# Routed attention: half of each head's weights turned by transfers, values one step later, the low halves of the rest on VectorE

## What is computed

```
ss = sigmoid(x @ Ws); sd = sigmoid(x @ Wd)            # two sets of gates, (b, t, H, E)
ms = _topk_mask(ss, 3); md = _topk_mask(sd, 3)        # three of five experts are kept
q = einsum('bthed,bthe->bhtd', q5, sd * md)           # q5 = x @ Wq, per head and expert
k = einsum('bthed,bthe->bhtd', k5, ss * ms)
v = einsum('bthed,bthe->bhtd', v5, ss * ms)
attn = softmax(einsum('bhid,bhjd->bhij', q * scale, k))
out = einsum('bhij,bhjd->bihd', attn, v)              # then spread over the experts by md and projected by Wo
```

## Time and profile before

| | |
|---|---|
| runs | 2855.82, 2860.48, 2865.31 us |
| profiled execution | 2857.4 us, span 2855.6 us |
| busy over the span | TensorE 88%, its weight load 59%, VectorE 72%, ScalarE 51%, GpSimd 65% |
| mean granted clock of TensorE | 0.951 |
| first scores of stage g0, of stage g1 | 1429.95 us, 2226.42 us after the start |
| step starts (scores of the next step) in g1 | 2249.90 (step 0) to 2821.48 (step 62) |

### The profile page before, as it was taken

The page is one execution under the profiler, slowest core; times in us unless marked ns, Lnnn a source line. Parts: engine busy times, 40 slices in busy tenths (PEclk is TensorE's granted clock), DMA queues, the critical chain, the costliest instruction groups (busy, mean ns, idle before and its releaser), DMA issues. The chain is left out here.

```text
span 2855.6 us, 59345 instructions
## 1 busy us (share of the span) xinstructions
PE 2525.9 (88%) x22659; PEld 1696.9 (59%) x22718; DVE 2049.0 (72%) x3682; ACT 1453.3 (51%) x2071; POOL 1853.3 (65%) x1754
## 2 busy tenths in 40 slices
PE   6787696795999999999689999999797899999997
PEld 3555444553666666666456666666534566666666
DVE  7998446446677677676688888887485888888874
ACT  4222122334888888888334455445362245544554
POOL 1887100003999999999357888887501577888885
PEclk9998798897999999999899999999898999999999
DMA  1000000003998998899300000000101000000000
GB/s 42 1 1 0 22 1 13 22 1 87 155 157 148 150 156 150 149 157 142 87 1 1 2 1 2 2 1 2 30 1 59 1 1 1 2 1 2 2 1 16
DMA packets 362421, 126.25 MB, mean 44 GB/s; under 512 B 344584, under 2 KB 353288, under 8 KB 362144
## 3 DMA queue, kind: packets, MB, share of 16 engines
q1 hardware_dynamic: 362144, 122.46, 23.3%
HBM read 20.70 MB, written 1.05 MB: 8 GB/s over the span
## 5 line engine op out<-in xcount | busy, mean ns | idle before, releaser
L2290 PE MATMUL banks<-g_w,normed_t 128*128 128x320 f32 x1536 | 498.6, 452 | 28.8 <-DVE g_scratch L2578 28.8
L1561 ACT COPY g_p_t<-banks 128x512 f32<-128x512 f32 x512 | 287.9, 588 | 398.9 <-PE banks L1532 398.0
L2578 DVE TENSOR_TENSOR g_scratch<-banks,g_gate 128x640 f32<-128x640 f32 x384 | 314.1, 821 | 191.3 <-PE banks L2290 188.1
L1767 DVE TENSOR_REDUCE at_negmax<-banks 128x1 f32<-128x1024 f32 x256 | 301.4, 1219 | 155.9 <-PE banks L1679 155.9
L1744 POOL TENSOR_TENSOR at_p_lo<-at_p,at_p_hi 128x640 bf16<-128x640 f32 x256 | 356.6, 1406 | 23.7 <-ACT at_p_hi L1732 21.6
L1591 POOL TENSOR_TENSOR g_p_lo<-g_p_t 128x512 bf16<-128x512 f32 x256 | 266.6, 1045 | 148.7 <-ACT g_p_t L1561 126.4
L2290 PEld LDWEIGHTS banks<-g_w,normed_t 128*128 128x128 f32 x1536 | 267.9, 193 | 120.7 <-DVE g_scratch L2578 46.8
L1574 ACT ACTIVATE g_p<-banks,g_negmax 128x1024 f32<-128x1024 f32 x256 | 286.2, 1118 | 101.3 <-DVE g_negmax L1579 93.8
L1579 DVE TENSOR_REDUCE g_negmax<-banks 128x1 f32<-128x1024 f32 x256 | 310.3, 1217 | 34.3 <-PE banks L1510 34.0
L1532 PEld LDWEIGHTS banks<-identity,g_p 128*128 128x128 f32 x2048 | 234.8, 141 | 138.6 <-issue 115.9
L1532 PE MATMUL banks<-identity,g_p 128*128 128x128 f32 x2048 | 295.9, 278 | 5.1 <-DVE g_p_lo L1585 2.9
(11 more groups left out here) (408 smaller groups left out, 5963.8 us busy)
## 6 DMA issues: line engine op xcount, KB each, us to landing
at_swapped<-at_crossed SPq DMA_DIRECT2D x128, 128.0 KB, 2.8
g_w<-in_ex_w SPq DMA_DIRECT2D x2, 2880.0 KB, 11.7
f_w<-in_W SPq DMA_DIRECT2D x2, 1024.0 KB, 5.7
at_rope<-in_rope SPq DMA_DIRECT2D x1, 2048.0 KB, 9.8
at_t_hi<-at_p_hi SPq DMA_TRANSPOSE x128, 3.6
at_t_lo<-at_p_lo SPq DMA_TRANSPOSE x128, 3.5
g_w<-in_ex_w SPq DMA_DIRECT2D x2, 960.0 KB, 5.0
out<-residual SPq DMA_DIRECT2D x1, 1024.0 KB, 5.1
```

The source lines that it names most:

```text
L1561: self.nc.scalar.copy(self.pt[:, j % self.deep, h, g * CHUNK:(g + 1) * CHUNK], self.core.ps[self.home(n)]).then_inc(self.pt_copied, 1)
L1767: self.nc.vector.tensor_reduce(self.negmax[:, j % 2, h:h + 1], self.core.banks[:, first:first + 2, :], AX.XY, ALU.max, negate=True).then_i ...
L2290: nc.tensor.matmul(out[:, 0:ED], core.xt[:, at:at + P], w[:, kind * H + tile // (T * BATCH) * 2 + h, :], start=True, stop=True).then_inc(p ...
L2578: v.tensor_tensor(qk_product[:, tile % 2, kind] if kind < 2 else v_product[:, tile % 2], core.banks[:, bank:bank + 2, 0:ED].rearrange("p h ...
```

## The change

- `__init__`: `home` in place of `homes`, no `on_pool`, `on_dve` and `deep`. New tiles `p_hi`, `p_lo` (bfloat16, first 512 columns of each head), `t_hi`, `t_lo` (turned by DMA), `u`, `u_lo` (turned by TensorE). All of them have two halves, used by turns.
- TensorE turns only the last four blocks of each head (`transpose(pe, j, h)`), both groups into bank 4 (in the last unit 4 and 6), each after VectorE has subtracted the group before (`u_split`).
- The first four blocks: ScalarE casts them to bfloat16 (`act_hi`), GpSimd subtracts (`pool_lo`, both operands in the untransposed layout), and SP issues for each step one DMA transpose of the high and one of the low halves (`turn`), 8 blocks of 128 by 128 each.
- ScalarE copies one group per head in place of two; VectorE's `dve_lo` does the low halves of both TensorE groups, as many as before.
- `values` of both heads are now of step j - 1, in step j; they wait for the transfers.
- The low halves of v move from GpSimd to VectorE (`dve_split_values`), the high halves to step t = 0 of the unit.
- The tiles of q and k of the next unit are turned into banks 0 and 1 in place of 6 and 7, and copied by ScalarE at the end of its step; the scores of the next step wait for that.
- The order of the work within a step is rewritten on every engine.

```diff
+    def act_hi(self, act, j, h):
+        act.wait_ge(self.exp_done, 2 * j + h + 1)
+        if j >= 2:
+            self.wait_turned(act, j - 2)
+        self.nc.scalar.copy(self.p_hi[:, j % 2, h, :], self.p[:, j % 2, h, 0:CHUNK]).then_inc(self.hi_ready, 1)
+
+    def pool_lo(self, pool, j, h):
+        pool.wait_ge(self.hi_ready, 2 * j + h + 1)
+        if j >= 2:
+            self.wait_turned(pool, j - 2)
+        self.nc.gpsimd.tensor_tensor(self.p_lo[:, j % 2, h, :], self.p[:, j % 2, h, 0:CHUNK], self.p_hi[:, j % 2, h, :],
+                                     ALU.subtract).then_inc(self.lo_ready, 1)
+
+    def turn(self, sp, j, part):
+
+        src, dst, ready = ((self.p_hi, self.t_hi, self.hi_ready), (self.p_lo, self.t_lo, self.lo_ready))[part]
+        sp.wait_ge(ready, 2 * j + 2)
+        if j >= 2:
+            sp.wait_ge(self.av_done, 2 * (j - 2) + 2)
+        sp.dma_start(dst[:, j % 2], src[:, j % 2].rearrange("p h n -> p (h n)"), transpose=True).then_inc(self.turned[j % 2], 16)
...
     def values(self, pe, j, h):
...
+        self.wait_turned(pe, j)
+        pe.wait_ge(self.u_split, 2 * j + h + 1)
...
@@ block.sync
+            for j in range(STEPS):
+                for part in range(2):
+                    hs.turn(sp, j, part)
@@ block.tensor, one step
                 if j + 1 < STEPS:
-                    if t == T - 1:
-                        pe.wait_ge(qk_ready, (unit + 1) * 4 + 4)
+                    if t in (3, 7) and unit + 1 < UNITS:
+                        pe.wait_ge(qk_ready, (unit + 1) * 4 + t // 4 * 2 + 2)
                     hs.scores(pe, j + 1)
...
+                hs.transpose(pe, j, 0)
...
                 beside(0)
-                hs.transpose(pe, j, 0, 1, STEPS)
                 if j:
+                    hs.values(pe, j - 1, 0)
+                beside(1)
+                hs.transpose(pe, j, 1)
...
+                if turning:
+                    pe.wait_ge(hs.exp_done, 2 * j + 3)
+                    for i in range(2):
+                        turn(unit + 1, t // 4 * 2 + i, core.ps[i])
...
+                if j:
                     hs.values(pe, j - 1, 1)
...
-                hs.transpose(pe, j, 1, 0, STEPS)
-                hs.transpose(pe, j, 1, 1, STEPS)
...
-                hs.values(pe, j, 0)
                 beside(2)
@@ block.scalar, one step
+                hs.act_copy(act, j, 0)
+                if not last:
+                    hs.act_exp(act, j + 1, 0)
...
+                if not last:
+                    hs.act_hi(act, j + 1, 0)
+                if t == 0 and unit:
+                    hs.act_split_values(act, unit, (v_ready, (unit + 1) * T - T // 2))
+                if not last:
+                    hs.act_exp(act, j + 1, 1)
+                hs.act_copy(act, j, 1)
+                if not last:
+                    hs.act_hi(act, j + 1, 1)
                 if t in (2, 6) and unit + 1 < UNITS:
                     for i in range(2):
-                        place(unit + 1, t // 4 * 2 + i, spare[i])
...
+                        place(unit + 1, t // 4 * 2 + i, core.ps[i])
@@ block.gpsimd, one step
-                hs.pool_lo(pool, j, 0, 0)
+                for h in range(2):
+                    hs.pool_lo(pool, j, h)
                 if j + LEAD - 1 < TOTAL:
                     sum_tile(j + LEAD - 1)
                 if j:
                     route(j - 1)
-                hs.pool_lo(pool, j, 1, 1)
@@ block.vector, one step
                 if j + 1 < STEPS:
                     hs.dve_max(dve, j + 1, 0)
                 beside(0)
+                hs.dve_lo(dve, j, 0)
                 if j + 1 < STEPS:
                     hs.dve_max(dve, j + 1, 1)
-                hs.dve_lo(dve, j, 0, 1)
-                if j:
-                    hs.dve_normalise(dve, j - 1, STEPS)
...
                 beside(1)
-                hs.dve_lo(dve, j, 1, 0)
-                beside(2)
+                if t == 0 and unit:
+                    hs.dve_split_values(dve, unit)
                 if j + T < TOTAL:
                     sum_values(j + T)
+                hs.dve_lo(dve, j, 1)
+                beside(2)
+                if j:
+                    hs.dve_normalise(dve, j - 1)
```

More of the change, by code:

```diff
@@ L1471, in __init__ @@
         self.exp_done = sem("exp_done")
-        self.pt_full = sem("pt_full")
-        self.pt_copied = sem("pt_copied")
-        self.pt_copied_dve = sem("pt_copied_dve")
-        self.lo_dve = sem("lo_dve")
-        self.lo_pool = sem("lo_pool")
+        self.hi_ready = sem("p_hi_ready")
+        self.lo_ready = sem("p_lo_ready")
+        self.turned = [sem(f"turned{i}") for i in range(2)]
+        self.u_full, self.u_copied, self.u_split = sem("u_full"), sem("u_copied"), sem("u_split")
         self.av_done = sem("av_done")
@@ L1481, in __init__, with wait_turned @@
         self.v_split = sem("v_split")
-    def wait_copied(self, eng, n):
-        on_dve = self.copied_on_dve[n % 4]
-        eng.wait_ge(self.pt_copied_dve if on_dve else self.pt_copied, sum(self.copied_on_dve[g % 4] == on_dve for g in range(n + 1)))
-    def groups_on(self, pool, last):
-        return sum(self.on_pool[g % 4] == pool for g in range(last + 1))
-    def home(self, n):
-        return self.homes(n // 4)[n % 4]
+    def wait_turned(self, eng, j):
+        eng.wait_ge(self.turned[j % 2], 32 * (j // 2 + 1))
     def fill(self, pool):
@@ L1502, in scores @@
             pe.wait_ge(self.exp_done, 2 * j)
-        if j >= 2 and min(self.homes(j - 2)) < 4:
-            for g in range(4):
-                self.wait_copied(pe, 4 * (j - 2) + g)
-            pe.wait_ge(self.lo_dve, self.groups_on(False, 4 * (j - 2) + 3))
         for half in range(2):
@@ L2176, in expert_attention_stage @@
         z_t = sb("z_t", [P, 3, P])
-        hs = HeadStream(core, ctx, tag, homes=lambda j: (4, 4, 0, 1) if j < TOTAL - T else (4, 6, 4, 6),
-                        on_pool=((0, 0), (1, 1)), sums=5)
+        hs = HeadStream(core, ctx, tag, home=lambda j, h: 6 if h and j >= TOTAL - T else 4, sums=5)
         STEPS = UNITS * T
@@ L2348, in beside @@
                         pe.wait_ge(product_ready, n // 2)
-                        if k == 1 and turning:
-                            pe.wait_ge(qk_ready, (unit + 1) * 4 + t // 4 * 2 + 2)
                         for h in range(2):
                             project(n + h, spare[h])
-                def finish(i, half):
-                    if unit + 1 == UNITS and i < len(done_in(t)):
-                        (turn_out if half == 0 else project_out)(*done_in(t)[i])
+                finishing = done_in(t) if unit + 1 == UNITS else ()
                 if j == STEPS - T:
@@ L2360, in _ @@
                 if j + 1 < STEPS:
[L2361 to L2362 removed]
+                    if t in (3, 7) and unit + 1 < UNITS:
+                        pe.wait_ge(qk_ready, (unit + 1) * 4 + t // 4 * 2 + 2)
                     hs.scores(pe, j + 1)
[L2364 to L2367 removed]
+                if unit + 1 == UNITS and t > 2:
+                    project_out(*done_in(t - 1)[1])
+                hs.transpose(pe, j, 0)
+                for k, tile in finishing[0:1]:
+                    turn_out(k, tile)
+                beside(0)
+                if j:
+                    hs.values(pe, j - 1, 0)
+                beside(1)
+                hs.transpose(pe, j, 1)
+                for k, tile in finishing[0:1]:
+                    project_out(k, tile)
+                if turning:
+                    pe.wait_ge(hs.exp_done, 2 * j + 3)
+                    for i in range(2):
+                        turn(unit + 1, t // 4 * 2 + i, core.ps[i])
+                for k, tile in finishing[1:2]:
+                    turn_out(k, tile)
                 if j:
                     hs.values(pe, j - 1, 1)
[L2370 to L2382 removed]
                 beside(2)
[L2384 removed]
+            project_out(*done_in(T - 1)[1])
+            hs.values(pe, STEPS - 1, 0)
             turn_out(*done_in(T)[0])
@@ L2438, in _ @@
                 hs.act_exp(act, 0, h)
+                hs.act_hi(act, 0, h)
             wait_values(act, T)
@@ L2628, in _ @@
                     sum_values(n // 2 - 2 * T)
+            hs.dve_split_values(dve, 0)
             for j in range(STEPS):
@@ L2659, in _ @@
                     keep(range(1, PAIRS), range(2 * T))
[L2660 removed]
+            hs.dve_normalise(dve, STEPS - 1)
             for t in (T, T + 1):
```

136 lines of the change are left out of this document (44 added, 92 removed).

## The result

The changed kernel took 2814.24 us (median of 4 runs, 2811.06 to 2817.76), the kernel before 2858.32 us (4 runs, 2855.82 to 2865.31): a ratio of 0.9833, interval 0.981 to 0.9857. A second set of runs beside the last experiments gave 0.9826 (0.9811 to 0.984). Forecast were 2788 us, 72.8 us saved; 44 are. The time lies in the range 2764 to 2848 and outside the likeliest case's own 2772 to 2803. The profiled execution took 2814.5 us with a span of 2812.7.

A forecast was written before the change was run, and what follows sets the result against it. TensorE was taken to set the pace, GpSimd close behind. Per stage 29.0 (steps 6 to 52) + 1.5 + 6.4 - 0.5 = 36.4 us, two stages 72.8 saved: 2787.7 us, range 2764 to 2848.

The forecast's parts named there:

- likeliest case: Whole kernel: the forecast of 2787.7 us itself, with its own range of 2772 to 2803 and a chance of 0.58.
- The ordinary step: Step without q and k turning: 8.28 us for 8.76, set by scores, first pair, four VectorE operations, third pair.
- the turning step: Step that also turns q and k blocks: 9.42 us, 0.65 saved, next scores waiting for ScalarE's placing.
- TensorE runs free: Rival: TensorE's two waits vanish, steps of 7.77 and 9.06 us, 2752 us in all; chance 0.08.
- The low half of v on VectorE at no cost: Once a unit, some 1.1 us (bounds 1.1 and 2.2) fits into VectorE's idle time.
- GpSimd at 1.1: Each GpSimd subtraction takes 1.1 us, its work 8.3 us a step in units 2 to 7.
- the second rival: GpSimd binds: subtractions of 1.386 us, steps of 8.9 in units 2 to 7, 2813 us; 0.15 with small-wait mixtures.
- The transfers: Two DMA transposes a step, 8 blocks each, land 3.5 us after issue and cost nothing.
- Steps 0 to 5: Start of a stage: VectorE, also choosing experts, sets the pace; 1.5 us saved, between 0 and 3.
- Steps 53 to 61: End of a stage: 66.9 us for 73.3, 6.4 saved, with 7.1 a step in steps 56 to 61.
- the loop: Low half, landing, values, normalising, routing, subtraction over two steps: allows 7.6 us a step, 7.1 in steps 56 to 61.
- The tail: Last maxima to last addition in a stage: 23.2 us for 22.7, 0.5 lost, now holding the last landing.

The follow-up runs named there:

- a2: Changed kernel with TensorE turning the four blocks of head 1 twice in each step: 2825.49 us, 0.9877.
- b1: Changed kernel with ScalarE placing the next unit's q and k ahead of the copy and high half of head 1 in turning steps: 2806.02 us, 0.9801.
- b2: Changed kernel with VectorE's low half of head 0 before the first gates and half of head 1's values before the second pair of projections: 2804.47 us, 0.9792.
- a1: Changed kernel with the low halves of v subtracted on GpSimd again, their high halves cast at the end of the unit before: 2823.73 us, 0.9872.
- a3: Changed kernel with a third, unused transposing transfer in each step, issued ahead of that of the low halves: 2830.3 us, 0.99.
- c0: The changed kernel unaltered, run and profiled again in the last set: 2812.48 us, 0.9826.
- c3: Changed kernel with all output tiles of the last unit moved behind step 63: 2904.05 us, one run.
- a4: Changed kernel with head 1's values, in the last unit only, ahead of the first output projection and second output tile's turning: 2809.01 us, 0.9815.
- b4: Changed kernel with b1, b2 and a4 together, and in the last unit each step's second output tile projected and added a step later: 2797.21 us, 0.977.
- c1: Changed kernel with GpSimd subtracting the low halves of step 63 before it routes step 61: 2811.73 us, 0.9823.

## Why the prediction was right, and where its size went

The direction and the mechanism were right: TensorE's blocks were the cost, and what is left of the step is the row that was laid out. The first and the last steps of a stage were not laid out as well, and that the total still came within 1% is in part luck: errors of 10.2 and 8.9 us stood against each other.

- **The ordinary step, 8.28, and the turning step, 9.42**: measured 8.30 to 8.31 and 9.42 to 9.43. a2, b1 and b2 moved what the layout named, and the steps followed. "TensorE runs free" is refuted by the waits on `g_scratch`.
- **The low half of v on VectorE at no cost**: wrong. Its own 1.1 us was right; what the forecast put at nothing is that it first waits for GpSimd's instruction, 1.36 to 2.01 us in all, and one step a unit is 0.5 to 0.8 longer. Six a stage, with 0.02 on each ordinary step, make most of the 5.1 us a stage that steps 6 to 52 fall short of the forecast. The Trainium skill, GPSIMD Engine Reference, its table with the SBUF interfaces, says that GpSimd contends with such an instruction. The trace agrees, with 2.28 us for 1.27 on GpSimd and 1.56 for an estimated 1.1 on VectorE. The bound of 2.2 had room for it, but the price was set at the low end, which just fits into the 1.1 us of idle time.
- **GpSimd at 1.1, the second rival at 1.386**: measured 1.16; its own work was 8.46 us a step in units 2 to 7. That is above the ordinary step and below the mean with a turning step in four (8.58). It doesn't bind: TensorE waits for a late transfer twice in 240 us, 0.9 us in all, and the waits on `g_scratch` and `g_k_t` set the steps. That the rival's 2813 is the time that was measured is chance; steps of 8.9 us aren't there. a1 adds 2.17 us a unit, and 8.3 us of waits for transfers come in the same stretch.
- **The transfers**: 3.2 us for 3.5; no wait in units 0 and 1, two in 240 us later, and a few of up to 2.4 us in the last unit and the tail. a3 shows the margin. The figure of the Trainium skill (VectorE: DVE Perf Modes, "The three transpose paths"), 1309 ns for one block, doesn't describe this transfer. Eight blocks land in 3.2 us, 0.4 each.
- **Steps 0 to 5, 1.5 us a stage**: mis-sized, 5.9 measured, and 4.6 in c0's profile, without the first stage's stretch at the full clock. I took VectorE as full there. Before the change it waited for TensorE for 11.6 of these 67 us (VectorE's waits, 2250 to 2317):

```profile
DVE g_scratch L2578 <- PE banks L2290: 9.5, 8, 2.7
DVE g_negmax L1579 <- PE banks L1510: 2.1, 1, 2.1
```

  and for 2.3 of 61.6 in the changed kernel (2227 to 2288.6):

```profile
DVE g_scratch L2565 <- PE banks L2279: 1.7, 3, 0.9
DVE g_negmax L1573 <- PE banks L1498: 0.6, 1, 0.6
```

  What fell away was TensorE's lateness, more than half of it as time.
- **Steps 53 to 61, 6.4 us a stage saved**: the step of the prediction that failed most. "Steps 56 to 61 have no gates, and there the loop decides: 7.1". Steps 53 to 55 came as laid out (24.4 us in c0, 24.3 forecast; 26.1 in the profile above, by the clock). The loop does allow 7.1 (c3: 6.76 and 7.2), but steps 56 to 61 also hold up to two output tiles each, which the forecast never priced, and these set 8.9. Before, the values of head 0 came last in the step and hid the tiles' waits; now two heads' values stand behind them. a4 and b4, 8.17 and 7.65, show this by the order alone. Of the 18.6 us that are missing over both stages some 13 are this and some 5 the lower clock of three steps.
- **The tail, 0.5 lost a stage**: 4.9 measured. In the second stage, from step 62's scores to the routing of step 62 were 12.7 us before (2821.48 to 2834.17) and are 17.9 now (2773.60 to 2791.50); after that both take 12 us to the last addition. In the first stage the same stretch is 12.7 and 15.6 us (1997.76 to 2013.33). The difference between the stages is the clock: over the first 10.4 us it is 1.00 in the first and 0.83 in the second, where the scores take 3.1 us and not 1.9. So 2.9 us are the order and 2.3 the clock; c0 has both again (27.7 and 29.8 us to the last addition, for 27.7 and 29.7). The values a step later put step 62's heads behind the output tiles of step 63; how the 2.9 us divide between the values' place and the tiles was not tried. The other 2.1 us of the first stage's 4.7 lie behind its last addition, in the stages in between (132.6 for 130.5 us, granted clock 0.89 for 0.91), which the change doesn't touch. The DMA that I named as the cost isn't on the path (c1).

The forecast of 2788 was 26 us too low, 30 by the spans; 18.6 us of it are steps 53 to 61 and 8.7 the tail, the 10.2 us in the middle are nearly paid by the 8.9 us at the start.

## What to carry to other kernels

Lay a new order out operation by operation along one step, with starts taken from the trace: it gave the steady state to 0.03 us. Do the same for the first and last steps, which hold other work: here the last unit and the tail made 27 of the 30 us. Before an error of a few microseconds is shared out among causes, read the granted clock of the stretches that are compared, or take a second profile: here it made some 7 of these 27 us (5 in the last unit, 2.3 in the tail), and made a tail look 1.7 us shorter that was not. When work moves a step later, ask what its new step holds ahead of it, and before removing a wait look for a second one that ends at the same moment.

## What the runs showed of the hardware

- A transposing DMA that is added to SP's queue delays the next by its issue, 1.23 us (up to 2.1 in the changed kernel and 2.6 in a3), and moves the time from issue to landing only from 3.2 to 3.4 us.
- VectorE's subtraction with both operands in SBUF (1040 columns, float32 and bfloat16, shown with 1.36 to 2.01 us) and GpSimd's sums take turns: it ends 1.09 to 1.11 us after the GpSimd instruction that ran when it started, in all 16 cases, and GpSimd's next one is longer by the wait, 2.28 us for 1.27. For a shorter sum 0.72 becomes 1.60. VectorE's operations that read PSUM keep their time beside the same GpSimd sums (gates 803 to 831 ns over all 384).
- TensorE's granted clock, between its two levels of 1.2 and 2.4 GHz, moves the time of the same work. In c3, behind a wait of 2.55 us, the scores take 2.93 us from start to start (next operation at 1961.46) where they took 1.92 in the step before, at a granted clock of 0.64 for this stretch and 1.00 for the 5.5 us before it:

```profile
1958.53 3.00 PE L1498 MATMUL banks<-g_k_t,g_q 64*128 64x512 f32 x8 [2.55 <-ACT g_p L1541]
1961.46 1.11 PE L1513 MATMUL banks<-identity,g_p 128*128 128x128 f32 x4
```
